# A cleared scratch field behind every indirect transfer, own steps for TensorE's loads of expert numbers, and the written order made anew

## What is computed

```python
x = x + 0.5 * _L0_ffn_ref(_layernorm(x), ...)      # int8-quantized 128x128 matmul
x = x + _L0_attn_ref(_layernorm(x), ...)           # conv, gated linear recurrence, gelu FFN of 512
x = x + 0.5 * _L0_ffn_ref(_layernorm(x), ...)
x = x + 0.5 * _L1_ffn_ref(_layernorm(x), ...)      # mixture of experts, first pass (p = 0)
x = x + _L1_attn_ref(_layernorm(x), ...)           # gated linear attention
x = x + 0.5 * _L1_ffn_ref(_layernorm(x), ...)      # mixture of experts, second pass (p = 1)
```

```python
probs = _sigmoid(jnp.einsum('bsh,eh->bse', x, Wr) + rb)
scores, idx = jax.lax.top_k(probs, 2)
cw = (jax.nn.one_hot(idx, 8) * scores[..., None]).sum(-2)
for e in range(8):
    out = out + cw[..., e:e + 1] * (silu(x @ Wg[e].T) * (x @ Wu[e].T) @ Wd[e].T)
```

## Time and profile before

| | before |
|---|---|
| median of 3 runs | 683.96 us (683.24 to 685.11) |
| span of the profiled execution (its own time; the page gives no other) | 692.3 us |
| TensorE busy | 600.1 us, 87% of the span |
| VectorE, GpSimd, ScalarE busy | 497.2, 419.3, 387.7 us |
| indirect transfers on GpSimd | 128 scatters, 142 stores |
| mean granted TensorE clock | 0.972 |

### The profile page before, as it was taken

How to read it: one execution, slowest core, us unless ns; L and a number is a source line. 1 busy time by engine, 2 the same in 40 slices (tenths; PEclk the granted TensorE clock), 3 DMA queues, 4 the chain that set the end, 5 groups by cost and what they waited for, 6 DMA issues and landing times.

```text
span 692.3 us, 14370 instructions
## 1 busy us (share of the span) xinstructions
PE 600.1 (87%) x4124; PEld 476.3 (69%) x4124; DVE 497.2 (72%) x1721; ACT 387.7 (56%) x1019; POOL 419.3 (61%) x445
## 2 busy tenths in 40 slices
PE   0366999999989998999897899999999999978974
PEld 0224565655666797888696686769879989857863
DVE  7997999978998865557224798989877766553335
ACT  2395968988766545444353728466565355533541
POOL 5276696488567777567643614553776575775552
PEclk9996999999999999999999999999999999999997
DMA  7999000001033355666768600124216556566796
GB/s 258 410 411 371 0 1 1 1 0 32 13 99 94 97 156 161 186 193 180 211 176 245 235 6 1 35 66 131 74 43 172 153 151 177 161 182 189 231 297 232
DMA packets 60125, 100.97 MB, mean 146 GB/s; under 512 B 10288, under 2 KB 28592, under 8 KB 59792
## 3 DMA queue, kind: packets, MB, share of 16 engines
q1 hardware_dynamic: 50832, 81.52, 38.5%
q0 software_dynamic: 8640, 17.84, 7.4%
q10 hardware_dynamic: 576, 0.69, 0.3%
HBM read 61.79 MB, written 38.23 MB: 144 GB/s over the span
## 4 chain that ended last, share of the span: by engine, by line
PE 43%; DVE 13%; DMA 9%; issue 6%; POOL 3%; SPq 2%; ACT 2%; POOLq 0%; DVEq 0%; ACTq 0%
PE bank L1083 13%; PE bank L1058 6%; PE bank L1296 5%; DMA tin<-rows_by_expert 3%; PE bank L969 3%; PE bank L955 3%; PE bank L944 2%; DMA hid<-rows_done 2%; DMA rows_done<-tout,tdst 2%; PE bank L1064 2%; DMA rows_done<-tout,tin 1%; POOL rows_by_expert L840 1%; DVE qt L417 1%; PE bank L312 1%; PE bank L307 1%
## 5 line engine op out<-in xcount | busy, mean ns | idle before, releaser
L840 POOL DMA_INDIRECT rows_by_expert<-xx,sidx x128 | 128.1, 1001 | 72.2 <-issue 34.0
L1083 PE MATMUL bank<-tint,twt 128*128 128x128 f32 x1136 | 151.8, 282 | 6.0 <-DVE thidt L1121 3.4
L1083 PEld LDWEIGHTS bank<-tint,twt 128*128 128x128 f32 x1136 | 141.1, 196 | 22.0 <-issue 12.3
L1132 POOL DMA_INDIRECT rows_done<-tout,tin x98 | 96.3, 983 | 57.5 <-ACT tout L1107 34.8
L1121 DVE TENSOR_TENSOR thidt<-tsil,bank 128x256 f32<-128x256 f32 x142 | 58.2, 418 | 95.8 <-ACT tsil L1099 74.1
L1099 ACT ACTIVATE tsil<-bank 128x256 f32<-128x256 f32 x142 | 53.9, 384 | 89.9 <-PE bank L1083 88.4
L1058 PE MATMUL bank<-e_dn,thidt 128*128 x568 | 90.6, 286 | 15.5 <-DVE thidt L1121 7.3
L1058 PEld LDWEIGHTS bank<-e_dn,thidt 128*128 128x128 f32 x568 | 76.8, 195 | 25.2 <-issue 24.8
L1107 ACT ACTIVATE tout<-bank,tin 128x128 f32<-128x128 f32 x142 | 50.2, 366 | 62.9 <-PE bank L1064 43.7
L1132 POOL DMA_INDIRECT rows_done<-tout,tdst x44 | 43.7, 993 | 49.0 <-ACT tout L1107 35.9
L1296 PEld LDWEIGHTS bank<-bufA,bufB 128*127 128x127 f32 (+6 forms) x448 | 47.7, 176 | 11.6 <-issue 6.7
(11 more groups left out here) (272 smaller groups left out, 1331.0 us busy)
## 6 DMA issues: line engine op xcount, KB each, us to landing
twt<-moe_gu SPq DMA_DIRECT2D x142, 256.0 KB
rows_by_expert<-tout SPq DMA_DIRECT2D x25, 715.0 KB, 20.0
tin<-rows_by_expert SPq DMA_DIRECT2D x142, 65.0 KB, 2.6
hid<-rows_done SPq DMA_DIRECT2D x12, 512.0 KB, 5.5
x<-x_in SPq DMA_DIRECT2D x8, 256.0 KB, 4.4
rows_by_expert<-xx,sidx POOLq DMA_INDIRECT x128
out<-x SPq DMA_DIRECT2D x8, 256.0 KB, 3.9
rows_done<-tout,tin POOLq DMA_INDIRECT x98
```

The lines of the kernel that those rows point to most:

```text
L840: pool.indirect_dma_start(out=rows_by_expert, out_offset=bass.IndirectOffsetOnAxis(ap=sidx[h][:, k:k + 1], axis=0), in_=xx[h][:, r, t, :], ...
L1083: m = pe.matmul(bank[UP_BANKS[p][j]][:, c * P:(c + 1) * P], weights[:, c * P:(c + 1) * P], tint[g % TURNS][:, :], start=True, stop=True)
L1132: pool.indirect_dma_start(out=rows_done, out_offset=bass.IndirectOffsetOnAxis(ap=dst, axis=0), in_=tout[:, g % RING, :], in_offset=None).t ...
```

## The change

Three edits. First, behind each of the 270 indirect transfers GpSimd clears a scratch field `pause` of 128x112 float32 and waits until the clearing has finished. Second, TensorE's register loads leave `x_io_tensor` and become steps of their own, `x_ids_tensor`, 19 in a pass, which stand in TensorE's list where its order puts them. Third, the lists of all five engines are written anew; apart from the 38 new steps each holds the same steps as before, most of them moved by one to three places and a few by ten to thirty (on VectorE `r_start_vector(1)` by 87).

```diff
+PAUSE = 112
...
+        pause = sb("pause", [P, PAUSE])
...
                 pool.indirect_dma_start(out=rows_by_expert, out_offset=bass.IndirectOffsetOnAxis(
                     ap=sidx[h][:, k:k + 1], axis=0), in_=xx[h][:, r, t, :], in_offset=None).then_inc(s_scat[h], 16)
+                pool_step(pool, pool.memset(pause[:, :], 0.0))
...
+        def x_ids_tensor(pe, p, j):
+            pe.wait_ge(s_table, WAVES * p + wave_of(j) + 1)
+            expert_pe.update(values_of(ENG.PE, etab[p], chunk_at(j), E_ROUTED))
+
         def x_io_tensor(pe, p, s):
...
                 j = s - LAG_DOWN
                 g = p * NT + j
-                if chunk_at(j):
-                    pe.wait_ge(s_table, WAVES * p + wave_of(j) + 1)
-                    expert_pe.update(values_of(ENG.PE, etab[p], chunk_at(j), E_ROUTED))
                 pe.wait_ge(s_thid, g + 1)
...
             pool.indirect_dma_start(out=rows_done, out_offset=bass.IndirectOffsetOnAxis(ap=dst, axis=0),
                                     in_=tout[:, g % RING, :], in_offset=None).then_inc(s_st[g % RING], 16)
+            pool_step(pool, pool.memset(pause[:, :], 0.0))
...
         @block.sync
         def _(sp_):
             k_loads_sync(sp_)
-            t_load_sync(sp_, 0, 0)
-            t_weights_sync(sp_, 0, 0)
-            t_load_sync(sp_, 0, 1)
-            t_weights_sync(sp_, 0, 1)
...
```

More of the change, by code:

```diff
@@ L1534, in _ @@
                 t_load_sync(sp_, 0, j)
-            for j in range(31, 36):
+            for j in range(32, 35):
                 t_weights_sync(sp_, 0, j)
@@ L1538, in _ @@
                 t_load_sync(sp_, 0, j)
-            for j in range(36, 39):
+            for j in range(35, 37):
                 t_weights_sync(sp_, 0, j)
@@ L1555, in _ @@
                 t_load_sync(sp_, 0, j)
-            for j in range(47, 51):
+            for j in range(47, 50):
                 t_weights_sync(sp_, 0, j)
@@ L1583, in _ @@
             c_fetch_sync(sp_, 1, 0)
-            for j in range(65, 67):
-                t_load_sync(sp_, 0, j)
[L1586 to L1593, removed]
+            for j in range(64, 66):
+                t_weights_sync(sp_, 0, j)
@@ L1633, in _ @@
[L1633 to L1644, removed]
+            t_weights_sync(sp_, 1, 26)
@@ L1645, in _ @@
+            t_load_sync(sp_, 1, 28)
+            for j in range(27, 29):
+                t_weights_sync(sp_, 1, j)
+            for j in range(29, 31):
+                t_load_sync(sp_, 1, j)
+            for j in range(29, 31):
                 t_weights_sync(sp_, 1, j)
@@ L1647, in _ @@
                 t_load_sync(sp_, 1, j)
-            for j in range(32, 34):
+            for j in range(31, 33):
                 t_weights_sync(sp_, 1, j)
@@ L1664, in _ @@
                 t_load_sync(sp_, 1, j)
-            for j in range(45, 48):
+            for j in range(47, 50):
                 t_weights_sync(sp_, 1, j)
@@ L1694, in _ @@
[L1694 removed]
+            for j in range(64, 66):
+                t_load_sync(sp_, 1, j)
+            t_weights_sync(sp_, 1, 63)
+            t_load_sync(sp_, 1, 66)
+            for j in range(64, 66):
                 t_weights_sync(sp_, 1, j)
[L1696 removed]
+            for j in range(67, 69):
                 t_load_sync(sp_, 1, j)
             t_weights_sync(sp_, 1, 66)
+            t_load_sync(sp_, 1, 69)
+            t_weights_sync(sp_, 1, 67)
@@ L2508, in _ @@
             r_scatter_gpsimd(pool, 6, 1, 3)
-            for j in range(28, 38):
+            for j in range(30, 38):
                 t_store_gpsimd(pool, 1, j)
@@ L2913, in _ @@
             g_turn_tensor(pe, 2)
-            x_io_tensor(pe, 0, 75)
+            for j in range(74, 76):
+                x_io_tensor(pe, 0, j)
             g_turn_tensor(pe, 3)
@@ new lines, in _ @@
+            e_gate_tensor(pe, 7, 1, 0)
+            x_ids_tensor(pe, 1, 41)
+            x_ids_tensor(pe, 1, 45)
+            x_up_tensor(pe, 1, 39)
+            x_io_tensor(pe, 1, 43)
+            x_up_tensor(pe, 1, 40)
+            x_ids_tensor(pe, 1, 49)
+            x_up_tensor(pe, 1, 41)
+            x_io_tensor(pe, 1, 44)
+            for j in range(42, 44):
+                x_up_tensor(pe, 1, j)
+            for j in range(45, 47):
+                x_io_tensor(pe, 1, j)
+            x_up_tensor(pe, 1, 44)
@@ L3184, in _ @@
+            x_up_tensor(pe, 1, 58)
+            x_io_tensor(pe, 1, 61)
+            for j in range(59, 61):
                 x_up_tensor(pe, 1, j)
@@ L3605, in _ @@
             g_query_scalar(act, 0)
+            for j in range(69, 71):
+                x_in_scalar(act, 0, j)
             g_query_scalar(act, 1)
```

2070 lines of the change are left out of this document (1033 added, 1037 removed).

## The result

| | before | changed |
|---|---|---|
| median | 683.6 us (4 runs, 683.15 to 685.11) | 767.53 us (4 runs, 766.45 to 769.18) |
| ratio, 95% interval | | 1.1225, 1.1203 to 1.1247 |
| span of the profiled execution | 692.3 us | 767.4 us |
| mean granted TensorE clock | 0.972 | 0.951 |

The change costs 84 us. Forecast were +3.5 us and a range that ended at 695: the sign was right, the size far off.

The account below looks back on a forecast made before the run. TensorE was taken as the bound from 400 to 600 us, with later waits on GpSimd's stores and scatters. Clearings +6.4, loads -2.9 and end 0 gave +3.5 us on 683.96: 687.5 us, own range 684 to 692, 8-in-10 range 677.5 to 695.

Parts of the forecast that it names:

- take 0.20: GpSimd: a clearing behind an indirect transfer adds 0.20 us to the 1.26 us from one transfer to the next.
- Both bounds (0 and 0.26): GpSimd's added us per transfer: 0 if the clearing fits into the gap, 0.26 by the sum of 1.52 us.
- 54 us of GpSimd's time: All 270 clearings at 0.20 us each, most of it hidden inside GpSimd's 70.7 us of waiting for `tout`.
- 26 and nine transfers: Unhidden GpSimd transfers: 26 in the second pass cost 4.6 us, nine in the first 1.8; together +6.4 us.
- the rival of 696 us: Slower still: GpSimd bounds both passes, 8.5 - 1.3 + 5 = +12 us; chance 0.12.
- All other moves of one to three places: Reordered steps cost nothing, covered by TensorE's ready work from 400 to 600 us; otherwise 0.4 to 1 us each.
- Net 5.4 - 2.5: TensorE's loads as own steps: 5.4 us idle time saved, 2.5 put back, -2.9 us; ends -6.6 and +1.
- The four loads in a row: TensorE, first pass, last unit's counts: three times 1.02 us uncovered, 3.1 us, of which half, 1.5, was counted.
- The end, costed at 0: Last tiles and additions: 4.4 to 5.2 us lost against 4.8 gained, so 0; ends -4 and +5.
- no wait of 5 us: Sign on VectorE: no such wait between the last products, and additions without a gap to the end.
- the last scatter of the second pass: Sign on GpSimd: some 4 us later than 621.62 us, with over 1.91 us idle before the last wave's first transpose.
- The rule of the Trainium skill: GpSimd against VectorE on shared ports: some clearings would wait for a whole VectorE instruction, but few; sum unchanged.

## Why the prediction was wrong

**"The transfer behind a small instruction is just what now stands everywhere, so I go by those rows and take 0.20."** This step failed for the stores (and for the first scatter of each unit). The earlier trace rows shows a scatter without a semaphore instruction. A store is two instructions, and in the earlier trace rows the first of them is already hidden: stores follow every 1.26 us as scatters do. I didn't ask what hides it. The wait for the clearing takes that cover away: 0.73 us a store, 0.19 a scatter (0.20 was right for these). Added up, 142 x 0.73 + 128 x 0.19 = 128 us of GpSimd's time, where I had 54. That is an estimate and rather too high, since a store that waits for `tout` anyway loses less. Both bounds (0 and 0.26) lay below 0.73.

**"For all 270 that is 54 us of GpSimd's time, most of it inside the 70.7 us of waiting."** With 26 and nine transfers counted as the exceptions, this failed too. With all distances at the costed 1.45 us (old order, the wait moved) the clearings cost 28.5 us, not 6.4. Three kernels in the old order give the price of GpSimd's time: 51 us added cost 28.5, 34 us (behind the 128 clearings stand 102 scatters at 0.19, 16 stores at 0.73 and ten times other work at 0.26) cost 19.3, and 128 us cost 78.7: 0.56 to 0.61 us for each us added. So there is no slack to fill first. My reading is that GpSimd's waits for `tout` are partly the echo of its own lateness, for they still are 41.6 us in the run with clearings alone, which adds more than they were; no run shows it by itself. That the loop over 12 buffers carries this was my first explanation, and 16 buffers refute it; the long waits of that run speak for the gates, where TensorE waits for scatters; shown is only that more buffers don't help. In the new order, whose tiles are late already, the first 51 us cost only 1.8 to 3.1.

**"It decides once the waits of GpSimd for `tout` vanish before the gates"**, the rival of 696 us: right that GpSimd's time decides, mis-sized by both steps above. The waits shrank but didn't vanish (31.1 us are left), as they need not for the loss.

**"All other moves of one to three places I cost at nothing; TensorE's store of work from 400 to 600 us covers them".** This failed by 33.5 us (own loads) to 42.8 us. The store of work is read from 400 us on, and some 28 us are lost ahead of it, where TensorE's longest idle time was 1.84 us and the new order makes one of 5.93 and 19 us more of idle time in all. The condition was in the text ("if it didn't, each would cost a wait as in the rows"), but no place of the first pass was looked at for it. Which moves make up the rest is open.

**The loads, "Net 5.4 - 2.5".** The gain was sized at twice what it is: in the old order, where nothing had to be put back, the loads gave 2.0 to 3.0 us and not 5.4. That this is near the net 2.9 is chance. They were worth 9.3 us in the new order, which stays open, and nothing in the changed kernel. The four loads in a row stop TensorE for 3.4 to 3.9 us, about the 3.1 that was said (with one load at that place it stood for 0.78 us); the changed kernel and the one without clearings:

```profile
318.33 0.71 PE L1062 MATMUL bank<-e_dn,thidt 128*128 x4 [3.39 <-issue]
```

```profile
313.32 1.22 PE L1059 MATMUL bank<-e_dn,thidt 128*128 x4 [3.86 <-issue]
```

**The end, costed at 0.** From the last product of a tile on (VectorE in the changed kernel, which answers to the earlier trace rows):

```profile
744.01 0.42 DVE L1125 TENSOR_TENSOR thidt<-tsil,bank 128x256 f32<-128x256 f32 x1 [0.82 <-ACT tsil L1103]
...
748.17 0.69 DVE L966 TENSOR_TENSOR ehid<-egate,bank 128x512 f32<-128x512 f32 x1 [3.60 <-issue]
...
761.91 0.69 DVE L1166 TENSOR_TENSOR x<-x,bufC 128x512 f32<-128x512 f32 x1 [3.11 <-DMA bufD<-rows_done]
762.63 0.69 DVE L1167 TENSOR_TENSOR x<-x,bufD 128x512 f32<-128x512 f32 x1
```

From the last product to the last addition it is 18.6 us (744.01 to 762.63); before, 10.9 (678.28 to 689.14). `ehid` comes 4.2 us behind that product, as costed, and no wait of 5 us stands between the last products, but the additions again wait for the last fetch, 3.11 us (2.53 before). No run took this part alone. As for the last scatter of the second pass, it starts at 689.06 us instead of 621.62, not 4 us later but 67; TensorE's idle time of 1.91 us ahead of the last wave's first transpose does not grow but is gone (that transpose is at 695.41 us), since the tiles ahead are late as well.

The rule of the Trainium skill (SBUF — State Buffer, "Who interferes with whom"), by which GpSimd can be blocked for a whole VectorE instruction in a two-port mode, again changes nothing: the 270 clearings of the changed kernel took 205 ns at the median and 211 at most, so none waited for VectorE; in the run with clearings alone one took 1285 ns. The 0.83 us ahead of a store are not in the clearing's duration but behind it.

## What to carry to other kernels

When a wait is added to an engine, look for the small instruction that comes next on it: a semaphore instruction that ran beside the one before is then in the open (a register instruction may be too; no run tried it), and the transfer behind it pays for both. Put the wait straight ahead of the instruction that needs it. Don't take an engine's waits in a pipeline for slack: price its added time at the whole of it until a run shows less (here 0.6), and check moves of an order in each stage, not by one stage's store of work.

## What the hardware showed

- A transfer straight behind a small instruction that it waits for starts after 0.28 us; with a semaphore instruction between that must wait too, after 0.83 us, whether the small one takes 0.12 or 0.20 us. A store started at least 0.74 us after its semaphore instruction had ended, in the kernel before, the changed one, the one with clearings alone and the one with the wait moved; with the wait behind that instruction the 0.74 us pass beside the transfer ahead.
- Where TensorE waited more, its matmuls were slower as well: with clearings alone the mean granted clock is 0.939 and TensorE busy for 625.7 us, against 0.972 and 600.1 us, for the same 4124 matmuls: 25.6 of the 69.3 us between those two spans. The two don't go in step: with 16 buffers it was 0.930 and 612.2 us.
- One chip took 795.61 us for the kernel before, which took 682.7 to 684.7 us on the others. The kernel with clearings and 16 buffers took the same on both kinds (764.50 and 763.35 us), that with clearings behind scatters alone 760.79 and 701.98 us. The granted clock was lower there for the kernel before (0.921 to 0.929 against 0.970 to 0.984) and for the scatters' kernel (0.941 to 0.950 against 0.970 to 0.973). What does this is open.
